# Linear attention with a mixture of experts: attention steps of two head pairs in place of one

## The reference

```python
h = _layernorm(x) * (1 + ca) + sa
a = jax.nn.sigmoid(h @ W_gate + b_gate)        # per head: q, k, v, a
S = a_t[..., None] * S + k_t[..., None] * v_t[..., None, :]
o_t = jnp.einsum('bhk,bhkv->bhv', q_t, S)      # scanned over the 256 tokens
x = x + ga * (out @ W_o)
h = _layernorm(x) * (1 + cb) + sb
logits = jnp.einsum('bsh,eh->bse', h, router_w) + routing_bias
scores, indices = jax.lax.top_k(jax.nn.sigmoid(logits), 2)
x = x + gb * (shared(h) + sum_over_2(score * expert(h)))
```

## Time and profile before

| | us |
|---|---|
| median of 3 runs (1349.03 to 1354.21) | 1349.91 |
| the profiled execution's own time | 1352.62 |
| its span, first to last instruction | 1350.3 |
| PE busy | 1275.8 (94%) |
| PE weight loads busy | 1059.4 (78%) |
| DVE busy | 1140.6 (84%) |
| ACT busy | 810.7 (60%) |
| POOL busy | 912.5 (68%) |

### The profile page before, as it was taken

How to read it: one execution, slowest core, us unless ns; L and a number is a source line. 1 busy time by engine, 2 the same in 40 slices (tenths; PEclk the granted TensorE clock), 3 DMA queues, 4 the chain that set the end, 5 groups by cost and what they waited for, 6 DMA issues and landing times. The chain is left out here.

```text
span 1350.3 us, 37745 instructions
## 1 busy us (share of the span) xinstructions
PE 1275.8 (94%) x10935; PEld 1059.4 (78%) x10935; DVE 1140.6 (84%) x3207; ACT 810.7 (60%) x2054; POOL 912.5 (68%) x1410
## 2 busy tenths in 40 slices
PE   6999999999999999999999999999999899999970
PEld 5888878888888888788888888888788788888860
DVE  7889898988989898989898898989895477887767
ACT  5666666666666666666666666666665354444420
POOL 3445667676777768686767677676866547777754
PEclk9999999999999999999999999999999999999985
DMA  8910202020120202020202112020202166656246
GB/s 248 243 58 16 75 18 88 20 84 33 71 82 21 104 0 104 12 92 16 88 20 83 35 69 88 16 104 0 105 15 99 50 186 194 195 179 180 69 154 220
DMA packets 88439, 119.21 MB, mean 88 GB/s; under 512 B 9652, under 2 KB 52327, under 8 KB 88384
## 3 DMA queue, kind: packets, MB, share of 16 engines
q1 hardware_dynamic: 79296, 101.47, 23.5%
q0 software_dynamic: 9088, 17.07, 3.7%
HBM read 50.29 MB, written 61.79 MB: 83 GB/s over the span
## 5 line engine op out<-in xcount | busy, mean ns | idle before, releaser
L1472 PE MATMUL bank<-h_hi,big 128*128 128x256 f32 x768 | 238.3, 310 | 3.2 <-DVE h_lo L979 2.9
L1128 DVE TENSOR_TENSOR_SCAN pairs<-pairs 128x128 f32<-128x128 f32 x512 | 233.1, 495 | 2.4 <-issue 0.4
L1548 PE MATMUL head_banks<-pairs 64*128 64x128 f32 x2048 | 225.9, 297 | 2.6 <-DVE A L1154 1.4
L1559 PE MATMUL bank<-A,shared 128*64 128x256 f32 (+1 forms) x2048 | 223.0, 339 | 0.2 <-POOL A L497 0.2
L497 POOL TENSOR_SCALAR_AFFINE_SELECT A<-A 128x256 f32<-128x256 f32 x256 | 114.7, 448 | 154.7 <-ACT A L799 153.6
L1473 PE MATMUL bank<-h_lo,big 128*128 128x256 f32 x768 | 216.4, 282 | 0.0
L1474 PE MATMUL bank<-h_hi,big 128*128 128x256 f32 x768 | 216.3, 282 | 0.0
L1132 DVE TENSOR_TENSOR_SCAN pairs<-pairs,cap 128x128 f32<-128x128 f32 x512 | 215.7, 461 | 0.0
L1154 DVE COPY_PREDICATED A<-causal,head_banks 128x384 f32<-128x384 int32 x256 | 150.4, 587 | 64.7 <-PE head_banks L1548 64.5
L1548 PEld LDWEIGHTS head_banks<-pairs 64*128 64x128 f32 x2048 | 155.5, 186 | 59.6 <-issue 41.3
L673 POOL DMA_INDIRECT y_dram<-pairs,y_row x156 | 156.1, 1001 | 67.8 <-issue 43.9
(11 more groups left out here) (202 smaller groups left out, 2822.0 us busy)
## 6 DMA issues: line engine op xcount, KB each, us to landing
rows_dram<-pad_row SPq DMA_DIRECT2D x17, 2112.0 KB, 8.0
ga_all<-rows_dram SPq DMA_DIRECT2D x39, 264.0 KB
pairs<-y_dram SPq DMA_DIRECT2D x16, 512.0 KB
pairs<-in_L_ffn_gate_w_dram SPq DMA_DIRECT2D x39, 128.0 KB
pairs<-in_L_ffn_up_w_dram SPq DMA_DIRECT2D x39, 128.0 KB
ga_all<-in_L_ffn_down_w_dram SPq DMA_DIRECT2D x39, 128.0 KB
mod_rows<-mod_rows_dram SPq DMA_DIRECT2D x32, 128.0 KB, 3.1
h_all<-h_tile SPq DMA_DIRECT2D x16, 256.0 KB
```

The source lines that it names most:

```text
L1128: v.tensor_tensor_scan(F[:, par, cols], ga_t[:, par, cols], ga_t[:, par, cols], 1.0, ALU.mult, ALU.min)
L1472: t.matmul(dst, hi, m_hi, start=True, stop=False)
L1548: last = t.matmul(S[:, h, c * P:(c + 1) * P], keys[rows, :], queries[rows, :], start=True, stop=True)
L1559: last = t.matmul(O[h * DK:(h + 1) * DK, k * P:T], v_sb[:, k, vcols], blocks.rearrange("p c t -> p (c t)"), start=(k == 0), stop=(k == CHU ...
```

## The change

A step now holds two head pairs (a "duo", u = 0 and 1); a round is eight steps s, four per sequence (e = s mod 4). Names: step d in all, `round_of_steps` in place of two calls of `body`.

```diff
+DUOS = PAIRS // 2
+NDUO = B * DUOS
+SEP = P + 1
+WIDE = 2 * CHUNKS * SEP
...
+        QKS = ctx.enter_context(nc.psum_tensor("qk_banks", [P, 2, 512], f32))
+        Z = ctx.enter_context(nc.psum_tensor("z_bank", [P, 512], f32))[:, :]
+        S = ctx.enter_context(nc.psum_tensor("score_banks", [P, 3 * 512], f32))
+        Y = ctx.enter_context(nc.psum_tensor("y_bank", [P, 512], f32))[:, :]
+        VO = ctx.enter_context(nc.psum_tensor("vo_bank", [P, 512], f32))[:, :]
+        QK = [QKS[:, 0, :], QKS[:, 1, :]]
+        LG, RANK, HT = VO[:, 0:PT * E], VO[:, 0:(PT + 1) * E], VO[:, 0:2 * P]
```

On POOL (removed lines are left out here and below):

```diff
+            def gates(d):
+                alone(s_te, d + 1)
+                if not (isinstance(d, int) and d == 0):
+                    alone(s_fg, d)
+                g.tensor_scalar(parts(gi_t)[:, :, 0:P], ex[:, :, :].rearrange("p u (c t) -> p (u c) t", c=CHUNKS), 1.0, 1.0, ALU.mult, ALU.add).then_inc(s_a, 1)
+                alone(s_th, d + 1)
+                g.tensor_scalar(parts(ga_t)[:, :, 0:P], th[:, :, :].rearrange("p u (c t) -> p (u c) t", c=CHUNKS), 0.5, 0.5, ALU.mult, ALU.add).then_inc(s_at, 1)
+            def growth(d):
+                alone(s_fg, d + 1)
+                g.tensor_tensor(grown[:, ds(d * 2, 2)], ends(G, 0), ends(G, 1), ALU.add).then_inc(s_gm, 1)
+            def mask_second_head(d):
+                alone(s_ax, d * 2 + 2)
+                for u in range(2):
+                    last = causal_half(A[:, 1, u, 0:3:2, :])
+                last.then_inc(s_pm, 1)
...
+                for s in range(2 * DUOS):
+                    half, e = s // DUOS, s % DUOS
+                    b, d = i * 2 + half, i * 2 * DUOS + s
+                    if e == 0 and not (last and half == 1):
                         inverse_std(b + 2)
+                    if s == 0 and three:
+                        scatter_rows(i - 2, s_fill, (i - 2) * 16, (6, 7))
+                    if s in (1, 2) and two:
+                        for n in range(2):
+                            logits_exp(i - 1, (s - 1) * 2 + n)
+                    if e == 3 and (half == 1 or one):
                         update_x(b - 1)
+                    if s == 4 and one:
                         inverse_std2(i)
+                    if s == 5 and one:
+                        h_rows((i - 1) * 2 + 1, i - 1, 1, i)
+                    if s >= 5 and two:
+                        scatter_rows(i - 1, s_fill, (i - 1) * 16, ((0,), (1, 2, 3), (4, 5))[s - 5])
+                    mask_second_head(d)
+                    if not (last and s == 2 * DUOS - 1):
+                        growth(d + 1)
+                    if not (last and s >= 2 * DUOS - 2):
+                        gates(d + 2)
+                    if s == 4 and one:
+                        h_rows((i - 1) * 2, i - 1, 0, i)
```

On ACT:

```diff
+            def exponents(d, p):
+                sc.wait_ge(s_z, d + 1)
+                if not (isinstance(d, int) and d == 0):
+                    sc.wait_ge(s_a, d)
+                for u in range(2):
+                    last = a.activation(ex[:, u, :], Z[:, u * T:(u + 1) * T], ACT.Exp, scale=-1.0, bias=neg_bg[:, p + u:p + u + 1])
+                last.then_inc(s_te, 1)
+            def tanh_of(d, p, u):
+                if u == 0 and not (isinstance(d, int) and d == 0):
+                    sc.wait_ge(s_at, d)
+                ins = a.activation(th[:, u, :], Z[:, u * T:(u + 1) * T], ACT.Tanh, scale=0.5, bias=half_bg[:, p + u:p + u + 1])
+                if u == 1:
+                    ins.then_inc(s_th, 1)
...
+            def carry_keys(d):
+                sc.wait_ge(s_kt, d + 1)
+                for u in range(2):
+                    last = a.activation(kx[:, u, :], kt[:, u, 0:P], ACT.Copy, scale=ends(F, 0)[:, u:u + 1])
+                last.then_inc(s_kx, 1)
+            def second_head(d):
+                sc.wait_ge(s_sx, d + 1)
+                blocks = A[:, 1, :, :, :].rearrange("p u c t -> p (u c t)")
+                a.activation(blocks[:, 0:2 * P], S[:, 6 * P:8 * P], ACT.Copy).then_inc(s_ax, 1)
+                a.activation(blocks[:, 2 * P:6 * P], S[:, 8 * P:12 * P], ACT.Copy).then_inc(s_ax, 1)
...
+                    if one or s > 0:
+                        copy_o(d - 1)
+                    if e == 1 and (half == 1 or one):
+                        copy_y(b - 1)
+                    second_head(d)
+                    if e == 1 and not (last and half == 1):
                         h_attention(b + 1, b + 2)
+                    if s >= 6 and one:
+                        copy_h(i, (s - 6) * 2)
+                    if ahead:
+                        exponents(d + 2, p)
+                        tanh_of(d + 2, p, 0)
+                        copy_v(d + 3, 1 if e < 2 else 0, e % 2)
+                    if not (last and s == 2 * DUOS - 1):
+                        carry_keys(d + 1)
+                    if ahead:
+                        tanh_of(d + 2, p, 1)
+                    if s == 4 and two:
                         write_first_expert(i - 1)
```

On DVE (`moments`, `normalise`, `choose`, `weigh`, `places` and the like are as before):

```diff
+            def scans(d):
+                alone(s_a, d + 1)
+                if not (isinstance(d, int) and d == 0):
+                    alone(s_gm, d)
+                    alone(s_kt, d)
+                v.tensor_tensor_scan(G[:, 0:WIDE - 1], gi_t[:, 0:WIDE - 1], cap[:, 0:WIDE - 1], 1.0, ALU.mult, ALU.min)
+                alone(s_at, d + 1)
+                if not (isinstance(d, int) and d == 0):
+                    alone(s_kx, d)
+                    alone(s_qt, d)
+                v.tensor_tensor_scan(F[:, 0:WIDE - 1], ga_t[:, 0:WIDE - 1], restart[:, 0:WIDE - 1], 1.0, ALU.mult, ALU.add).then_inc(s_fg, 1)
+            def products(d):
+                alone(s_fg, d + 1)
+                alone(s_qk, d + 1)
+                for out, off, wide, signal in ((kt, T, G, s_kt), (qt, 0, F, s_qt)):
+                    v.tensor_tensor(out[:, :, :].rearrange("p u (c t) -> p u c t", c=CHUNKS),
+                                    QKS[:, :, off:off + T].rearrange("p u (c t) -> p u c t", c=CHUNKS),
+                                    wide.rearrange("p (u c x) -> p u c x", u=2, c=CHUNKS)[:, :, :, 0:P], ALU.mult).then_inc(signal, 1)
+            def first_head(d):
+                alone(s_sx, d + 1)
+                blocks = A[:, 0, :, :, :].rearrange("p u c t -> p (u c t)")
+                mask = causal[:, :, :].bitcast(i32).rearrange("p c t -> p (c t)")
+                v.copy_predicated(blocks[:, 0:4 * P], mask[:, 0:4 * P], S[:, 0:4 * P])
+                alone(s_ax, d * 2 + 1)
+                v.copy_predicated(blocks[:, 4 * P:6 * P], mask[:, P:3 * P], S[:, 4 * P:6 * P]).then_inc(s_am, 1)
...
+                    first_head(d)
+                    if not (last and s == 2 * DUOS - 1):
+                        products(d + 1)
+                    if s == 0 and two:
+                        logits(i - 1)
+                    if e == 0 and more:
+                        normalise(b * CHUNKS + CHUNKS, s_rs, b + 2, s_xn)
+                    if e == 1 and more:
                         split_h((1 - half) * T, b + 2)
+                    if s == 3 and two:
+                        choose(i - 1)
+                        weigh(i - 2, i - 1)
+                    if s == 3 and one:
                         moments2(b - 1, 1, i)
+                    if s == 4 and two:
                         places(i - 1)
+                    if s == 4 and one:
+                        for u in range(2):
+                            normalise2((i - 1) * 2 + u, u, i)
+                    if s == 7:
                         moments2(b - 1, 0, i + 1)
+                    if e == 3 and not last:
+                        if isinstance(b, int) and b == 0:
+                            dve.wait_ge(s_x_rest, 16)
+                        moments(b * CHUNKS + 2 * CHUNKS, b + 3)
+                    if not (last and s >= 2 * DUOS - 2):
+                        scans(d + 2)
```

On PE; the projections, `scores`, `attend` and `output` do for two pairs what they did for one, and attend now comes first in a step, then scores, projections, values, output:

```diff
+            def scores(d):
+                pe.wait_ge(s_kt, d + 1)
+                pe.wait_ge(s_qt, d + 1)
+                pe.wait_ge(s_kx, d + 1)
+                for u in range(2):
+                    for c, (keys, queries) in enumerate(blocks):
+                        if u == 1 and c == 1:
+                            pe.wait_ge(s_bank, d + 1)
...
                 last.then_inc(s_sx, 1)
...
+            def attend(d, e, values_copied):
+                pe.wait_ge(s_am, d + 1)
+                pe.wait_ge(s_ax, d * 2 + 2)
+                pe.wait_ge(s_pm, d + 1)
+                pe.wait_ge(s_v, values_copied)
...
+                    begun = one or s > 0
+                    ahead = not (last and s >= 2 * DUOS - 2)
+                    if begun:
+                        attend(d - 1, (e - 1) % DUOS, d + 2 if not (last and s == 2 * DUOS - 1) else NDUO)
+                    scores(d)
+                    if ahead:
+                        pe.wait_ge(s_th, d + 2)
+                        if e == 2:
                             pe.wait_ge(s_hl, b + 2)
```

(62 more changed lines are left out.)

445 lines of the change are left out of this document (160 added, 285 removed).

## The result

| | before | after |
|---|---|---|
| median of four runs each, us | 1349.47 | 1458.83 (1457.31 to 1460.96) |
| ratio, 95% interval | | 1.0805 (1.0791 to 1.0819) |
| profiled execution's own time, its span | 1352.62, 1350.3 | 1457.31, 1455.2 |
| one round (steady, 200 to 900 us) | 62.6 | 70.1 to 70.3 |

The change makes the kernel 8.05% slower, 109 us. Slower was forecast, by 76 us; 1458.83 lies just above the range, whose end was 1458.

The account below looks back on a forecast made before the run. PE's instruction stream in the attention stage was taken as the bound. Per round 55.4 + 5.9 + 0.3 + 4.6 + 1.1 + 0.7 = 68.0 against 62.6, 76 us more in all: 1426 us, range 1390 to 1455, widened to 1338 to 1458.

Parts of the forecast that it names:

- five short stands with transposes and router: PE in steps 0, 1, 5, 6 and 7, waiting for the shared bank to be read: 5.9 us per round.
- PE's gain: PE's phases of two pairs together: fewer phase switches, 6.93 us in place of 7.46, so 4.2 less per round.
- rival 4: Switch cost sits in each pair's first matmuls, not in the phase; PE keeps 59.7 us a round: 1485 us, chance 0.05.
- The shared bank: One bank for values, attend outputs and transposes; PE waits for its readers before values, 5.9 us per round with work.
- Step 4: PE waits after ranks for DVE's in-order list, 11.9 us against PE's own 7.35: a stand of 4.6 per round.
- Rival 1: DVE's list of steps 3 and 4 fits within PE's 7.35 us; no long stand: 1336 us, chance 0.20.
- Step 5: Attend waits for GpSimd's mask behind rows and scatter: chain 10.9 us, PE there after 9.8, so 1.1 more (0 to 2).
- The clock: PE's clock halves after step 4's stand: costs 1.5 us, 0.8 hidden under the mask wait, so 0.7 per round (0 to 2).
- Rounds and ends: 14 routing rounds add 5.4 us each, 76; rounds 0 and 1 save 3 together; start and end add 3.
- Rival 2: As forecast, but PE's clock stays up after the stand: 67.3 us per round, 1416 us, chance 0.13.
- thin slack: Experiments' rival theory: wide single-buffered steps leave so little slack that a removed wait comes back elsewhere; no chance given.
- the list: Experiments' starting theory: the loss is PE's step-4 wait for DVE's in-order list, with clock and step 5's mask behind it.

Follow-up runs that it names:

- e8: Kernel after, with the gate projections put between the scores of a step's two pairs, adding two phase changes per step on PE: 1493.8 us.
- e4: Kernel after, with PE's stand of step 4 filled by 38 unused matmuls to keep the clock up: 1462.2 us.
- e6: Kernel after with the edits of e1, e2 and e3 together: 1357.4 us.
- e12: e10 with GpSimd's second h_rows and all scatters put between the two halves of gates: 1345.2 us.
- e1: Kernel after, with router logits, ranks and transposes moved from the bank of values and attend outputs to the third score bank: 1424.5 us.
- e2: Kernel after, with choose moved to step 2 and the next sequence's moments one step earlier on DVE: 1435.7 us.
- e3: Kernel after, with GpSimd's mask of step 5 put ahead of the second h_rows and the scatter: 1443.1 us.
- e11: e10 with GpSimd's mask, growth and gates ahead of the second h_rows and all scatters in every step: 1393.9 us.
- e10: e6 plus, on ACT in the four steps with transposes, the copy of values ahead of the exponents: 1342.9 us, ratio 0.9944 to the kernel before.
- e5: Kernel after with the edits of e3 and e4 together: 1435.2 us.
- e7: Kernel after with e1's edit, DVE's small work dealt out evenly, and GpSimd's mask and gates ahead of rows and scatters: 1382.6 us.
- e9: e1's bank and e7's DVE order, GpSimd's small work behind mask and gates over all eight steps, ACT's values copy earlier in transpose steps: 1404.9 us.

## Why the prediction was right and where it was not

| per round, us | forecast | measured |
|---|---|---|
| eight steps of PE without waits | 55.4 | 55.3 (8 x 6.91) |
| five short stands with transposes and router | 5.9 | 6.5 |
| ranks and the stand on next_row | 4.9 | 5.25 |
| step 5 and the clock | 1.8 | 3.2 |
| sum | 68.0 | 70.2 |

- **PE's gain** was right, 6.93 against 6.91, and e8 confirms that it is the edges of phases (against rival 4).
- **The shared bank**: each stand as forecast to 0.2; missed was that the first value matmul after a stand starts its successors late (0.80 for values in place of 0.70, five times).
- **Step 4**: DVE's list was added up to 11.9 and measured 12.16, PE's part to 7.35 and measured 7.27 (6.92 up to the ranks, 0.35 for them). The wait is the one forecast, on next_row. Rival 1 needed a list of 8.4.
- **Step 5, the price of GpSimd's rows: the step that failed.** The wait for the mask was the right mechanism, but its chain was mis-sized. From the first values to attend of step 5 the prediction put 10.9 (its terms add to 10.8) and PE's own path at 9.8; with 0.7 for the clock that makes 1.8. The chain takes 13.07, and PE's path up to the mask at full clock about 9.9: 3.2. In e4, at full clock, the chain still takes 12.19, 2.3 more than PE's path, where 1.1 was put: 1.2 of the 1.4 that is missing. It is the two h_rows on GpSimd, which were priced at 3.8 from the mean of the kernel before and take 5.1. The first multiplication takes 1.71 beside DVE's scans and 0.73 in the second h_rows, where none runs; e6 shows the same pair, 1.70 and 0.72, and in e12 the second takes 1.66 as soon as a scan runs beside it. The Trainium skill ("SBUF — State Buffer", "Who interferes with whom") says that a VectorE instruction with two inputs in SBUF contends with a GpSimd instruction that reads SBUF; the scan is one, and the 1.71 beside it against 0.73 agrees.
- **The clock** was nearly right. PE loses 1.9 by it in the round shown (values 0.75, output 0.86, attend 0.32) where 1.5 was put, and 1.0 of that runs under the wait for the mask, where the prediction had 0.8. What is left is what the late copy of values adds to the chain: 13.07 - 12.19 = 0.9, where 0.7 was put.
- **Rounds and ends**: 14 x 2.2 = 31 on 1426 gives 1457. The two profiled spans differ by 104.9 and 14 rounds by 106, so rounds 0 and 1 and both ends come to -1 where 0 was forecast; the medians differ by 109.4, which leaves 4.5 to the spread between executions.
- **The range** had bounds of 0 to 2 for the mask, 0 to 2 for the clock and up to 6 for the stand. All three at their upper ends are 1426 + 14 x (0.9 + 1.3 + 1.4) = 1476; it stopped at 1458. The three terms came out at 2.3, 0.9 and 4.9: the first lies beyond its bound, and the late starts after the five stands (0.5 a round) had none.
- **Rival 2** (the clock stays up) is refuted by the 0.50. The Trainium skill ("TensorE: Matmul & The Clock Gate", "Part 1: The HAM clock gate") has an idle engine fall back to the slow clock; behind the stands of 4.9 the trace agrees, with 0.50; the stands of the last section agree in part only.
- **The theory itself** was too narrow in one point. The prediction told the stall as one wait on one list. e1 removes that wait and recovers 34 us of 109; with e2 and e3 it is 101, where the three alone add up to 73. That speaks for one chain (DVE's list of steps 2 to 4, GpSimd's variances, DVE's rows, GpSimd's rows ahead of the mask), which PE met in several places; thin slack was the better name for what single edits do, and the list for where it starts.

## What to carry to other kernels

Halving the number of steps leaves the small work as it was and the places for it half as many: add up each engine's in-order list between two of the waits of the engine that bounds the kernel, step by step, not its busy share per round. Where a late list reaches the bound engine by two ways, removing one wait shows the other; edit the chain as a whole before judging it. Price an instruction with what will run beside it: a mean from the old order made the term that failed. In an in-order queue independent work belongs ahead of a wait, not behind it (e11 against e10 and e12).

## What the hardware showed that was not expected

The length of a stand did not decide alone whether the clock fell. In e5 it is 0.50 behind a stand of 1.31 us (above), but 1.00 behind most stands of that length; in e4 it fell behind most stands of 2.1; in e2, behind stands of 3.1 to 3.2, it stays at 1.00 in five rounds of eleven. In e7 it stays at 1.00 behind one of 2.71, though behind the ten like it before that the mean of the next 3 us was 0.50 to 0.70:

```profile
917.24 1.52 PE L1638 MATMUL vo_bank<-A,shared 128*64 128x256 f32 x16 [2.71 <-POOL A L512]
```

```profile
917.24:921.00 3.76, 3.76 (x46) 3.20 (x47) 3.26 (x5) 1.25 (x3) 3.29 (x4) 1.00 0.05 18
```

In e9 it stays at 1.00 behind two stands of 3.7 and 3.9 and falls behind the ten others of 3.7 to 4.1. What sets them apart was not tried.

A scan of 515 columns took 1.20 to 1.23 us undisturbed (1.04 to 1.3 was the bound), where two of 128 had taken 0.74. Beside GpSimd it is not always GpSimd that is late: in e11 a scan and an h_rows multiplication both start at 317.06, and there the multiplication takes its 0.72 and the scan 1.81.
